# Second attention of a two-block transformer kernel: values taken for four heads at a time instead of two

## The reference, cut to what matters

```python
q = (x @ wq).reshape(B, N, H, hd)          # H = 32 heads of hd = 8
k = (x @ wk).reshape(B, N, J, hd)          # J = 8 key/value heads
v = (x @ wv).reshape(B, N, J, hd)
q = _rope(q, ROPE_THETA); k = _rope(k, ROPE_THETA)
k = jnp.repeat(k, rep, axis=2); v = jnp.repeat(v, rep, axis=2)   # rep = 4
...
scores = jnp.einsum('bhqd,bhkd->bhqk', q, k) / jnp.sqrt(jnp.float32(hd))
scores = jnp.where(causal[None, None], scores, -jnp.inf)
weight = jax.nn.softmax(scores, axis=-1)
out = jnp.einsum('bhqk,bhkd->bhqd', weight, v)
return out.transpose(0, 2, 1, 3).reshape(B, N, D) @ wo
```

## Time and profile before

| | |
|---|---|
| median of 3 runs | 1107.75 us (1104.6 to 1109.08) |
| profiled execution, time | 1115.46 us |
| profiled execution, span of the core | 1113.6 us |
| PE busy | 946.8 us (85%) |
| DVE busy | 804.9 us (72%) |
| ACT busy | 566.4 us (51%) |
| mean granted TensorE clock | 0.95 |

### The profile page before, as it was taken

One profiled execution on the slowest core, in us unless ns is written; L12 is line 12 of the kernel. 1 busy time (PEld: TensorE's weight loads), 2 busy tenths in 40 slices (PEclk: granted clock), 3 DMA queues, 4 the chain that ended last, 5 costly groups with the idle time before them and its releaser, 6 DMA issues.

```text
span 1113.6 us, 18547 instructions
## 1 busy us (share of the span) xinstructions
PE 946.8 (85%) x6288; PEld 676.7 (61%) x6288; DVE 804.9 (72%) x2140; ACT 566.4 (51%) x1446; POOL 186.1 (17%) x168
## 2 busy tenths in 40 slices
PE   2899889988898889879889888868988997799993
PEld 2677667766676667654456565642333336688883
DVE  7689878987898879894277878466776776256554
ACT  2398529862886279731133333125665771445541
POOL 1101020102010201027323333300000005021111
PEclk9999999999999989979999999988999998699997
DMA  9999920000000000034287888424545653778773
GB/s 246 197 217 232 235 69 1 1 1 2 1 2 1 1 1 2 1 107 162 80 266 248 271 275 280 146 86 142 200 155 184 223 185 120 271 272 309 272 275 123
DMA packets 73326, 163.12 MB, mean 146 GB/s; under 512 B 11392, under 2 KB 53007, under 8 KB 69009
## 3 DMA queue, kind: packets, MB, share of 16 engines
q1 hardware_dynamic: 67568, 149.24, 44.6%
q0 software_dynamic: 5664, 12.71, 3.1%
HBM read 131.40 MB, written 62.19 MB: 174 GB/s over the span
## 4 chain that ended last, share of the span: by engine, by line
PE 54%; DVE 22%; DMA 9%; ACT 8%; issue 5%; SPq 1%; another core or an unknown queue 0%; POOL 0%; ACTq 0%; POOLq 0%; DVEq 0%
PE ps L1725 50%; DMA made<-arena 4%; DMA arena<-in_w0all 3%; DVE arena L1475 2%; DVE arena L1134 2%; DVE arena L1704 2%; DVE arena L1151 1%; ACT arena L656 1%; DVE arena L1143 1%; ACT arena L641 1%; DVE arena L1167 1%; DVE den L991 1%; DVE arena L1105 1%; ACT arena L634 1%; DVE arena L1702 1%
## 5 line engine op out<-in xcount | busy, mean ns | idle before, releaser
L1725 PE MATMUL ps<-arena 128*128 128x128 f32 (+15 forms) x4700 | 739.3, 333 | 64.6 <-DMA arena<-in_w0all 17.2
L1725 PEld LDWEIGHTS ps<-arena 128*128 128x128 f32 (+8 forms) x4700 | 505.6, 149 | 228.8 <-issue 99.6
L1475 DVE TENSOR_REDUCE arena<-ps 128x4 f16<-128x1024 f32 (+1 forms) x48 | 58.9, 1228 | 50.5 <-PE ps L1725 50.4
L1167 DVE SCALAR_TENSOR_TENSOR arena<-arena 128x128 f32<-128x128 f32 x240 | 84.1, 413 | 0.5
L1702 DVE CAST arena<-arena 128x128 f16<-128x128 f32 (+1 forms) x128 | 32.8, 256 | 67.1 <-ACT arena L870 57.2
L656 ACT ACTIVATE arena<-ident,arena 128x128 f32<-128x128 f32 x256 | 81.0, 391 | 0.0
L496 POOL TENSOR_TENSOR den<-den,backd 128x512 f32<-128x512 f32 x8 | 10.4, 1305 | 393.4 <-DVE euv L972 393.4
L870 ACT ACTIVATE arena<-ps,arena 128x128 f32<-128x128 f32 (+1 forms) x128 | 48.1, 418 | 49.1 <-PE ps L1725 44.4
L775 ACT ACTIVATE arena<-ps 128x1024 f32<-128x1024 f32 x48 | 49.2, 1024 | 43.3 <-PE ps L1725 43.3
L528 POOL DMA_INDIRECT made<-arena x47 | 53.0, 1127 | 107.8 <-DVE arena L1388 106.4
L1134 DVE SCALAR_TENSOR_TENSOR arena<-arena,ps 128x128 f32<-128x128 f32 (+1 forms) x128 | 47.2, 410 | 26.9 <-PE ps L1725 20.4
(11 more groups left out here) (296 smaller groups left out, 1263.1 us busy)
## 6 DMA issues: line engine op xcount, KB each, us to landing
arena<-split SPq DMA_DIRECT2D x15, 2048.0 KB
arena<-in_w0all SPq DMA_DIRECT2D x47, 608.0 KB
slots<-in_blank SPq DMA_DIRECT2D x17, 1040.0 KB, 19.6
arena<-in_w1all SPq DMA_DIRECT2D x16, 1024.0 KB, 6.9
split<-arena SPq DMA_DIRECT2D x32, 512.0 KB, 3.4
slots<-in_blank SPq DMA_DIRECT2D x10, 1044.0 KB, 22.7
arena<-slots SPq DMA_DIRECT2D x47, 130.0 KB
side<-made SPq DMA_DIRECT2D x8, 512.0 KB, 7.2
```

Source lines behind the costliest of these rows:

```text
L1167: ins = dve.scalar_tensor_tensor(dst, prob[:, n % 3, tiles[tt]], w, dst, ALU.mult, ALU.add)
L1475: dve.tensor_reduce(out, ps[:, at:at + 2].rearrange("p j (r s) -> p j r s", r=nr), X, ALU.max, negate=True).then_inc(max1_done, 1)
L1725: return pe.matmul(o, l, r, start=start, stop=stop, skip_group_check=shared)
```

## The change

`values(i, kind)` takes all four heads of a pass at once, in the four groups of 32 columns, instead of two. For that the probabilities of both pairs are made in turn: the order of steps in `scoresT` goes kind by kind (kind 0 of pair 0, kind 0 of pair 1, kind 1 of pair 0, ...). `values` is called behind steps 2 and 4 and at the pass's end, three times in place of six, with twice the multiplies in each. The semaphore `pv1_pe` counts three a pass in place of six, and ScalarE's waits on it are rewritten to match. `scores`, the maxima and everything else keep their order.

```diff
@@ ScalarE: exps1, outputs_out
                 if u >= 4:
-                    act.wait_ge(pv1_pe, u - 3)
+                    act.wait_ge(pv1_pe, (u - 4) // 2 + 1)
...
-                act.wait_ge(pv1_pe, 6 * i + 6)
+                act.wait_ge(pv1_pe, 3 * i + 3)
@@ TensorE: scoresT
-                jp, kind = divmod(k, 3)
+                kind, jp = divmod(k, 2)
@@ TensorE: values
-            def values(i, k):
+            def values(i, kind):
...
-                u = 6 * i + k
-                pe.wait_ge(exp1_done, u + 1)
-                if k == 0 and i:
+                pe.wait_ge(exp1_done, 6 * i + 2 * kind + 2)
+                if kind == 0 and i:
                     pe.wait_ge(oraw_read, i)
                 for rp in ((kind,) if kind < 2 else (0, 1)):
-                    for j in range(2):
-                        g = 2 * jp + j
-                        o, p = ps[32 * g:32 * g + 32, 4 + rp], probT1[:, u % 4, j]
+                    for g in range(4):
+                        o, p = ps[32 * g:32 * g + 32, 4 + rp], probT1[:, (6 * i + 2 * kind + g // 2) % 4, g % 2]
@@ TensorE: the loop over passes and steps
-                    if k:
-                        values(i, k - 1)
+                    if k in (2, 4):
+                        values(i, k // 2 - 1)
...
-                values(i, 5)
+                values(i, 2)
```

## The result

The changed kernel takes 1116.8 us in the median of 9 runs (1112.25 to 1125.72) against 1107.75 of the kernel before (9 runs): a ratio of 1.0088, with an interval of 1.0064 to 1.0111. It is slower by 9 us, not faster by 3. The profiled execution's span is 1117.1 us.

The account below looks back on a forecast made before the run. The bound was taken to change from step to step, TensorE also waiting for the exponentials and maxima. Gains of 0.9 + 2 x 0.6 + 0.65 + 4 x 0.1 = 3.15 us took 1107.75 to 1104.6, range 1099 to 1112.

Parts of the forecast that it names:

- What bounds the kernel: In the eight passes, the bound changes from step to step; TensorE savings count only where everybody waits for TensorE.
- the price of a call: A four-head `values` call takes 1.00 us, against 0.98 for two heads; 24 calls replace 48.
- Rival B: In `values`, four groups don't all work at once and a call takes 1.85 us: 1116 us in all; 12 in 100.
- The walk: Through the stage's passes, every step moved by what it waits for; 1103 to 1107 us, 55 in 100.
- passes of half 0: Passes 2 and 4: of a saving of 2.9 us, 0.6 arrives in each, as VectorE sets the later pace.
- pass 6: Nothing to rotate; `turn_o`, the router's inputs and the last maxima pace it: 0.65 us gained.
- pass 0: No `turn_o`, TensorE at its lower level; projection starts at 759.3 in place of 760.2: 0.9 us gained.
- half 1: Passes 1, 3 and 5: later steps wait for the exponentials and maxima, so only 0.1 us each is gained.
- rival C: New TensorE waits bring two to four more 3.3 us half-speed stretches, each losing at most 1.6: 1105 to 1111; 13 in 100.
- The sum of 3.15 us: Whole stage: 0.9 + 2 x 0.6 + 0.65 + 4 x 0.1 us gained, giving 1104.6 against the median.
- 20 of the 23 us turn into waits of TensorE: Of 23 us taken off TensorE's work in the stage, 20 become its waits for the exponentials and maxima.
- Rival D: Odd passes give 1 us each instead of 0.1 if ScalarE's and VectorE's pieces slide forward: 1099, best 1095; 20 in 100.

Follow-up runs that it names:

- e1: Changed kernel with the calls of kinds 0 and 1 made a second time, at steps 3 and 5; ratio to before 1.0043, stage 171.1 us.
- e8: Changed kernel with kind 1's call alone made a second time, at step 5 ahead of `turn_maxed`; one run, stage 169.4 us.
- e9: Kernel before with the calls of kinds 0 and 1 made cheaper by multiplying upper halves as bfloat16; ratio to before 1.0043, stage 179.1 us.
- e5: Changed kernel with its two inner calls at steps 3 and 5 in place of 2 and 4; ratio to before 0.9960, stage 161.7 us.
- e10: e5 with kind 1's call once more in passes of half 0, ahead of the last scores; ratio to before 1.0006, stage 164.1 us.
- e11: e5 run a second time, beside the kernel before; ratio to before 0.9946, stage 170.6 us.

## Why the prediction was wrong

**What bounds the kernel, and the price of a call: right.** The bound changes from step to step, and four groups work side by side at 1.00 us a call. Rival B (1.85 us) is refuted by the timeline.

**The walk: right in what it walked.** It had 0.6 us for passes of half 0. From the exponential of step 0 to that of step 3 pass 4 takes 12.55 us in the changed kernel and 13.18 before. It had 0.65 for pass 6, where the same piece takes 8.86 us in place of 9.48, and 0.9 for pass 0, where the projection starts 8.1 us behind the first exponential in place of 9.1. For half 1 at full clock it had 0.1, and e1 shows 17.7 against 17.8. But what passes 0 and 6 had gained was lost again at the lower level (pass 0's projection took 4.1 us in place of 2.7), and each of the two is 0.9 us longer than before.

**The step that failed is the clock: the sum put it at nothing, and rival C priced it too low.** The prediction had the mechanism and took it as an exception of 13 in 100: "two to four" more stretches of 3.3 us, with at most 1.6 us lost in each, and 1105 to 1111 us as the result. Measured were some 42 us more at 1.2 GHz, a stretch of 10 us and one of 3.4 in each of three pairs of passes, and more in passes 0, 6 and 7; passes 1, 3 and 5, which were to gain 0.1 us each, lost 2.7 to 2.8. Two mistakes lie in it. It counted stretches by the one wait that had been seen ahead of one, though the change also took out the call ahead of `turn_maxed`, and the walk itself says that `turn_maxed` then starts "with the maxima's end": the second wait was in the walk and its effect was not priced. And it let a stretch end after 3.3 us as before, where with the second wait it lasted 10; with one call put into that wait it ended after 3.4 us again (e8).

**The sum of 3.15 us** is thus not off in its terms, as far as they could be read; it lacks one, of about +12 us by the runs (9 + 3.15) and +15 by the stage (11.7 + 3.15). "20 of the 23 us turn into waits of TensorE" was told as free of cost. e1, e8 and e9 show that it was not.

**Rival D** put 1 us for each pass of half 1 on the pieces sliding forward. The changed kernel did not get it, and e5 did, from the place of the calls.

**Not settled:** why the same instructions at times keep the clock and at times lose it (pass 3 and pass 5 of e9, pass 3 and pass 5 of e10, pass 5 of e5 and of e11), and what brought the stretches in passes 6 and 7 (3.3 of the stage's 11.7 us). How the loss divides between less work and the new gap is not settled either: e9 lost time with less work and no call moved, and e8 got most of it back with one call more, in the gap. The runs show only that kernels with less TensorE work in this stage stand close to that edge.

## What to carry to other kernels

Where a stage's pace is set by other engines and TensorE has short gaps between calls, price what its work protects: making its calls cheaper can lower its clock, and then the calls that are on the path cost nearly twice. Put lumped work into the waits that are already there, and not ahead of what others await; here the same three calls a pass cost 5 to 10 us with the inner two at steps 2 and 4 and gained 4 to 6 with them at steps 3 and 5. And read the granted clock of the stage in both profiles before explaining a difference by order or by waits.

## What the runs showed of the hardware

Four groups of 32 columns work at once on float32 multiplies of four different operands: 1.00 us for four heads against 0.98 for two, and 1.86 us at the lower clock (pass 0 of the changed kernel, from 756.41). The first records of the four heads start within 20 ns, their second records 453 ns later (the call at 765.90). At the end of pass 4 the low level of the clock began just behind a wait of 2.3 us and 2.55 us, before and in the changed kernel. It lasted 10 us in the changed kernel, where a second wait of 1.3 us followed, and 3.4 us in e8, where a call of 1.0 us stood in the place of that second wait. In e9 a whole pass of 25.5 us ran at 1.2 GHz with TensorE recorded busy 24.9 of 26.2 us: at the lower level records are longer, so this high busy share was no sign that the clock would rise.
